# Moving the on-chip bases of an attention and mixture-of-experts kernel to multiples of 512 bytes

## The reference, cut to what matters

```python
x = x + attn(layernorm(x), Wq, bq, Wqa, bqa, Wk, bk, Wka, bka, Wt, bt)
# attn: softmax-pooled query, keys scaled by it, softmax-pooled key,
#       (pooled_k * mixed_q) @ Wt + bt + mixed_q
h = rmsnorm(layernorm(x)) * norm_weight
shared = relu(h @ sw1 + sb1) @ sw2 + sb2               # 256 -> 1024 -> 256
probs = sigmoid(h @ router_w.T)                        # 8 experts
scores, idx = top_k(probs, 2)
w = scores / (sum(scores) + 1e-6)
routed = sum over the two of w * (relu(h @ ew1[e] + eb1[e]) @ ew2[e] + eb2[e])
x = x + shared + routed
```

## Time and profile before

| | |
|---|---|
| median of 3 runs | 714.48 us (712.64 to 715.02) |
| the profiled execution | 713.45 us |
| its span in the profile | 711.7 us |
| TensorE products busy | 696.7 us, 98% of the span |
| VectorE, ScalarE, GpSimd busy | 533.0, 443.6, 184.8 us |
| data moved by DMA | 107.02 MB, mean 150 GB/s |

### The profile page before, as it was taken

One profiled execution on the slowest core, in us unless ns is written; L12 is line 12 of the kernel. 1 busy time (PEld: TensorE's weight loads), 2 busy tenths in 40 slices (PEclk: granted clock), 3 DMA queues, 4 the chain that ended last, 5 costly groups with the idle time before them and its releaser, 6 DMA issues.

```text
span 711.7 us, 13039 instructions
## 1 busy us (share of the span) xinstructions
PE 696.7 (98%) x4972; PEld 622.8 (88%) x4972; DVE 533.0 (75%) x1026; ACT 443.6 (62%) x745; POOL 184.8 (26%) x155
## 2 busy tenths in 40 slices
PE   8899899999999999999999999999999999999998
PEld 6457687999899898999898989998989989898887
DVE  6756898988657759785877678859766877757886
ACT  3643488436746869466848584769485775866532
POOL 2100110000021435353435253435332643121000
PEclk9999999999999999999999999999999999999999
DMA  8500131030014645474565455745544666424773
GB/s 296 222 2 1 60 114 65 1 126 2 1 30 149 226 156 182 173 254 150 181 220 173 156 194 189 272 141 189 179 156 149 202 223 214 149 82 140 242 247 104
DMA packets 41262, 107.02 MB, mean 150 GB/s; under 512 B 9357, under 2 KB 25744, under 8 KB 33648
## 3 DMA queue, kind: packets, MB, share of 16 engines
q1 hardware_dynamic: 34384, 88.49, 37.4%
q0 software_dynamic: 6816, 17.71, 7.5%
HBM read 89.39 MB, written 17.69 MB: 150 GB/s over the span
## 4 chain that ended last, share of the span: by engine, by line
PE 86%; DVE 7%; ACT 3%; issue 1%; DMA 1%; POOL 1%; SPq 0%; DVEq 0%; ACTq 0%; POOLq 0%
PE psD L734 13%; PE psD L735 13%; PE psD L741 13%; PE psU L711 12%; PE psU L707 11%; PE psU L705 11%; PE psT L655 2%; PE psU L526 1%; PE psU L679 1%; PE psU L681 1%; PE psU L678 1%; PE psT L628 1%; DVE hlo L1409 1%; PE psU L690 1%; DMA x_sb<-in_x 1%
## 5 line engine op out<-in xcount | busy, mean ns | idle before, releaser
L1028 ACT ACTIVATE hid<-psU,b 128x512 f32<-128x512 f32 (+2 forms) x280 | 152.8, 580 | 132.2 <-issue 83.2
L734 PE MATMUL psD<-w,hhi 128*128 128x256 f32 x824 | 198.6, 282 | 0.5 <-DVE hhi L1405 0.4
L735 PE MATMUL psD<-w,hhi 128*128 128x256 f32 x824 | 195.2, 278 | 0.0
L1409 DVE TENSOR_TENSOR hlo<-hid,hhi 128x512 fp32r<-128x512 f32 x206 | 139.5, 691 | 53.2 <-ACT hhi L1031 50.4
L734 PEld LDWEIGHTS psD<-w,hhi 128*128 128x128 f32 x824 | 155.1, 188 | 1.4 <-issue 0.6
L735 PEld LDWEIGHTS psD<-w,hhi 128*128 128x128 f32 x824 | 155.2, 188 | 0.5
L1456 DVE TENSOR_TENSOR w<-raw,w 128x1024 fp32r<-128x1024 f32 x112 | 133.3, 1218 | 3.0 <-ACT w L907 2.5
L438 POOL DMA_INDIRECT xin<-token_in,src x71 | 80.8, 1139 | 206.6 <-DVE src L1655 99.4
L446 POOL DMA_INDIRECT token_out<-fold,dst x71 | 90.6, 1276 | 160.6 <-DVE fold L1450 152.2
L711 PE MATMUL psU<-xhl,w 128*128 128x512 f32 (+1 forms) x448 | 125.0, 360 | 0.0
L705 PE MATMUL psU<-xhl,w 128*128 128x512 f32 (+1 forms) x448 | 125.0, 360 | 0.0
(11 more groups left out here) (222 smaller groups left out, 650.6 us busy)
## 6 DMA issues: line engine op xcount, KB each, us to landing
raw<-in_wpack SPq DMA_DIRECT2D x58, 1024.0 KB
xT<-token_out SPq DMA_DIRECT2D x32, 256.0 KB, 3.4
token_in<-z_sb SPq DMA_DIRECT2D x8, 512.0 KB, 2.9
out<-x_sb SPq DMA_DIRECT2D x16, 256.0 KB, 3.9
b<-in_b2pack SPq DMA_DIRECT2D x29, 128.0 KB
x_sb<-in_x SPq DMA_DIRECT2D x6, 512.0 KB, 6.8
xin<-token_in,src POOLq DMA_INDIRECT x71
token_out<-fold,dst POOLq DMA_INDIRECT x71, 5.1
```

The costliest lines, as they stand in the source:

```text
L734: mm(acc, hhi[:, part], whi[slot][:, c * D:(c + 1) * D], start=(c == 0), stop=False)
L735: mm(acc, hhi[:, part], wlo[slot][:, c * D:(c + 1) * D], start=False, stop=False)
L1028: last = nc.scalar.activation(hid[:, n % 4, i * rows:(i + 1) * rows], acc, ACT.Relu, bias=b1[:, u % 2, m:m + 1])
L1409: V.tensor_tensor(hlo[:, part], hid[:, n % 4, :], hhi[:, part].bitcast(F32), ALU.subtract).then_inc(hlo_ready, 1)
```

## The change

Two unnamed tensors are taken that nothing reads or writes: 96 floats (384 bytes a partition) ahead of `x_sb`, and 40 floats (160 bytes) ahead of `raw`. `b1` (64 bytes) is taken ahead of `raw` instead of behind `w`. The table `iota` is held once (8 columns) instead of 32 times (256 columns), so that `cst` and the array on the host have 248 columns less; both readers see the one row through an access pattern that repeats it 32 times. The instruction at L1516 gets three-dimensional operands in place of flat ones. No instruction is added or taken away, and the order of all of them stays.

The bases of the tensors that carry the work (`x_sb`, `xT`, `w3`, `cst`, `raw`, `w`, `b2`, `b2s`, `xin`, `fold`, `xhl`, `hid`, `hhi`, `hlo`, and `z_sb`, `att` early on) become multiples of 512 bytes. From the paddings and sizes, before the change `x_sb`, `xT`, `w3` and `cst` start at 128 past a multiple of 512, `raw` and `w` at 384 past one, and all from `b2` on at 448 past one.

```diff
-C_SCAN = C_IOTA + NT * E
+C_SCAN = C_IOTA + E
...
+        sb("ahead_of_rows", [P, 96])
         x_sb = sb("x_sb", [P, NT, D])
...
+        b1 = sb("b1", [P, 2, MH])
+        sb("ahead_of_raw", [P, 40])
         raw = sb("raw", [P, 2, W2])
...
-        b1 = sb("b1", [P, 2, MH])
         b2 = sb("b2", [P, 2, D])
...
-        iota = cst[:, C_IOTA:C_IOTA + NT * E].rearrange("p (t e) -> p t e", e=E)
+        iota = cst[:, C_IOTA:C_IOTA + E].rearrange("p (o e) -> p o e", o=1).to_broadcast([P, NT, E])
...
-                link(V.scalar_tensor_tensor(line(ra), line(ra), -float(E), iota.rearrange("p t e -> p (t e)"),
-                                            ALU.mult, ALU.add))
+                link(V.scalar_tensor_tensor(ra[:], ra[:], -float(E), iota, ALU.mult, ALU.add))
...
-    c[:, C_IOTA:C_IOTA + NT * E] = np.tile(np.arange(E), NT)
+    c[:, C_IOTA:C_IOTA + E] = np.arange(E)
```

## The result

The changed kernel takes 723.38 us (median of 6 runs, 722.94 to 725.73) against 714.75 us; the ratio is 1.0127, with a 95% interval of 1.0098 to 1.0156. It is slower by 1.3%. The forecast was no change, 714.5 us, in a range of 707 to 720: wrong.

The account below looks back on a forecast made before the run. TensorE, busy 98% of the span, was taken as the bound. Pace, table and transfers each added 0 to the 711.7 us span (713.45 with 1.75 outside it), so the median was forecast again: 714.5 us, range 707 to 720.

Parts of the forecast that it names:

- what bounds the kernel: Whole kernel: TensorE, products busy 98% of the span; only its pace and short stretches at start and end could matter.
- the table costs 0: Four instructions at L1516 and L1520 reading the expert-number table: 0.42 us each, change 0, at most 0.24 us.
- the shorter second transfer and the landings: Start of kernel: `cst` landing 1.5 us earlier, not waited for, 0; first-row landing taken as 0, bounds -1.7 and +1.4 us.
- VectorE's instructions don't feel the base: 112 writings of a weight's rest, 1214 to 1227 ns at both bases: no base effect, 0.
- the rule of the Trainium skill: First rows' transfer: 2 KB pieces starting 128 bytes off need 9 transactions, not 8; estimated 0.6 us earlier, sum unchanged.
- this term: TensorE's pace in `up` and `down` matmuls: effect of moved bases taken as 0, ends -6.7 and +12.6 us.
- rival 2: TensorE matmuls: equal bases modulo 512 make loads and moving reads clash, slower; 727.1 us full, 720.8 half; chance 0.20.
- full price of +12.6 us: `down` and B `up`: 1896 matmuls slow by 4.5 ns, 8.5 us; 960 wide ones by 4.3 ns, 4.1 us.
- the larger cost: 256-column matmuls: even the fast pace carries 6.8 ns above 106.7; 512 columns carry 15.7, so none expected back.
- The reading that the number of transposes ahead of a block fits its pace: Between `up` and `down`: A before B slow with 4 transposes, A before C fast with 2; a question of timing.
- the two ends of an unknown term: TensorE's pace: best -6.7 us, matmuls at fast paces; worst +12.6 us, narrow and wide ones at slow paces.

Follow-up runs that it names:

- the paddings: Changed kernel with 32 to 256 unused bytes ahead of `b2`, in steps of 32, moving `b2` and later bases: 714.94 us (64 bytes) to 729.69 us (160).
- turn5: Kernel before the change, with one transpose more ahead of the `down` that precedes a B block, same value written again: 713.82 us, ratio 1.0002.
- turn6: Kernel before the change, with two transposes more ahead of the `down` that precedes a B block, same value written again: 714.25 us, ratio 1.0017.
- iota_alone: Kernel before the change with only the table held once, its freed bytes kept unused so other bases stay: 713.4 us, ratio 0.9987.

## Why the prediction was wrong

**Right:** what bounds the kernel; that only TensorE's own pace could move the end; that the table costs 0 (0.43 for 0.42 us, and the run with it alone at 0.9987); that the shorter second transfer and the landings count for nothing; that VectorE's instructions don't feel the base (1215 to 1227 ns for 1214 to 1227). On the rule of the Trainium skill that I had weighed, which tells of reads (DMA: Bandwidth & Descriptors, "How a descriptor splits into AXI transactions"): the estimated gain of 0.6 us in the first landing did not come (5.45 us for 5.42).

**The step that failed** is "I take 0 for this term, since the only two bases compared agree". The two bases, 128 and 384 past a multiple of 512, are 256 bytes apart, and 256 is the period: they could not disagree. I had written exactly this down as what the trace cannot show, and that the change moves the distance between the two operands by 64 bytes, and still took the agreement as evidence. An experiment that varies a quantity by one whole period of the possible effect says nothing about the effect. The term measured +10.6 us of matmuls in place of 0. One pair of rows did compare two distances: the `up` of A (229.0 ns) has the moving operand 64 bytes past the stationary one, that of C (233.3), where `xhl` is the stationary operand, has it 64 bytes short of it. The prediction read both rows and did not set them against each other; the paddings show that most of it goes with the distance (at 0 it is 227.4 and 229.0).

**The rival that came true** is the second, which had 0.20: more cost where all bases are equal modulo 512. What it named, the relative base of the two operands, is what the runs show; that the two clash in the memory, none of them shows. Its figures were off both ways. Every 256-column matmul went to 120 ns, a third pace slower than the 118 that I had as the worst; the wide ones did not go to 233 but got faster, 227.4. Its full price of +12.6 us came out near the +10.6 measured by two errors of opposite sign (11.4 + 1.0 of narrow matmuls for the 8.5 named, -1.8 of wide ones for +4.1). The reason for expecting nothing back of the larger cost, that what lies above 106.7 ns grows with the columns and so is not the operand's start, was also too simple: at distance 0 the excess is 13.3 ns for 256 columns and 14.1 for 512, nearly the same for both. The reading that the number of transposes ahead of a block fits its pace fell with `turn5`, `turn6` and `iota_alone`.

The range ended at 720 because half of rival 2's weight was left outside it, and the result lies in that half; with the two ends of an unknown term at -6.7 and +12.6 us and nothing that told the middle from the ends, it should have reached to the upper one.

## What is shown and what is open

Shown: the mean pace, and with it the time, follows the distance between the bases of stationary and moving operand, modulo 256 bytes and with its sign; the price is paid where the pair of operands has the distance, and partly in the stretch behind it. Argued only: that it is the next weight load that meets the current moving read. The Trainium skill (SBUF — State Buffer, "Who interferes with whom") gives TensorE two read ports that are independent, one for the moving operand and one for weight loads, and says that TensorE never waits on anyone. The runs sit badly with this: with nothing changed but the distance, the mean of the same fp32r matmuls goes from 115.2 to 119.8 ns, though no run shows a port that waits. Open: whether and where the two reads meet in the memory, whether the price falls to a matmul's own load or to the next one's, and what picks the pace of a stretch where there are two.

## What to carry to other kernels

In this kernel, where TensorE is the bound and loads weights for each matmul, the bases of its two operands relative to one another were worth 1 to 2% (714.9 to 729.7 us by padding alone). In one like it, try a few paddings of 32 or 64 bytes and read the distance between starts in the chain of work. Rounding all bases to one multiple sets that distance to 0, which for 256 columns of fp32r was, with +96, the slowest place seen. When a trace offers an accidental comparison, ask first whether the two cases differ in the thing that the change moves.

## What the runs showed that I had not expected

The distances (moving minus stationary base) are not ordered by size: for 256 columns +64 and -64 take 117.3 to 117.9 and 114.8 to 115.3 ns, 128 takes 118.6 to 118.9, 0 takes 119.8 to 120.0, +96 takes 119.9; for 512 columns (S and A) 0 is the best (227.4), then +64 (229.0), and all others lie at 232.4 to 234.1. At +64 and at -64 there are two stable paces for 256 columns, 113.5 and 118 ns, and most blocks keep the one that they start with, for up to a hundred matmuls; two runs of the same bases can differ in which one a block has.
